# Linear attention and its neighbours: a split wait, a gate and half a unit in other places, the router's scores behind the first Silu

## What is computed

```python
# ffn0, on the layer-normed tokens xf
shared = jax.nn.silu(xf @ shared_w1.T) * (xf @ shared_w2.T) @ shared_w3.T
scores = jax.nn.sigmoid(xf @ router_w.T)
_, top_idx = jax.lax.top_k(scores + expert_bias, TOP_K)
...
return (shared + routed).reshape(b, s, d)

# gla, H = 4 heads, q/k of 64, v of 128 per head
q = split(x @ Wq.T, HQK); k = split(x @ Wk.T, HQK); v = split(x @ Wv.T, HV)
g = jax.nn.log_sigmoid((x @ Wgk1.T @ Wgk2.T + bgk2) * GATE_MULT) / GATE_NORM
o = gla_fused_chunk(q, k, v, g)      # S_t = diag(exp(g_t)) S_{t-1} + k_t v_t^T ; o_t = q_t^T S_t
o = o * jax.lax.rsqrt(jnp.mean(o * o, axis=-1, keepdims=True) + EPS) * rms_w
gate = jax.nn.silu(x @ Wg.T)
return o.reshape(B, N, DV) * gate @ Wout.T
```

## Time and profile before

| | us |
|---|---|
| timed runs, median (lowest to highest of 3) | 1657.66 (1654.03 to 1658.09) |
| profiled execution | 1649.87 |
| its span, first to last instruction | 1647.8 |
| PE busy | 1604.7 |
| DVE, ACT, POOL busy | 1181.8, 875.4, 706.5 |
| share of the chain that ended last: PE | 83% |

### The profile page before, as it was taken

How to read it: one execution, slowest core, us unless ns; L and a number is a source line. 1 busy time by engine, 2 the same in 40 slices (tenths; PEclk the granted TensorE clock), 3 DMA queues, 4 the chain that set the end, 5 groups by cost and what they waited for, 6 DMA issues and landing times.

```text
span 1647.8 us, 42417 instructions
## 1 busy us (share of the span) xinstructions
PE 1604.7 (97%) x15094; PEld 1082.7 (66%) x15095; DVE 1181.8 (72%) x2536; ACT 875.4 (53%) x1509; POOL 706.5 (43%) x660
## 2 busy tenths in 40 slices
PE   6999999999999999999999999999999999999998
PEld 3665566666666776765655666666657777777576
DVE  6677775666666666667866656666688879888886
ACT  5455543444376666664343334444376676675664
POOL 2342242433235455442332333334235567777343
PEclk9999999999999999999999999999999999999999
DMA  7132233333311211003210123333423033231001
GB/s 263 52 102 88 87 103 92 110 110 111 93 31 27 38 26 25 0 1 88 100 43 26 38 78 100 112 109 105 106 62 53 2 79 80 54 67 42 20 32 52
DMA packets 91304, 115.71 MB, mean 70 GB/s; under 512 B 9425, under 2 KB 76529, under 8 KB 91185
## 3 DMA queue, kind: packets, MB, share of 16 engines
q1 hardware_dynamic: 70832, 71.17, 15.2%
q0 software_dynamic: 20352, 42.88, 9.1%
HBM read 66.11 MB, written 47.90 MB: 69 GB/s over the span
## 4 chain that ended last, share of the span: by engine, by line
PE 83%; DVE 7%; ACT 5%; issue 3%; POOL 1%; DMA 1%; DVEq 0%; SPq 0%; ACTq 0%; POOLq 0%
PE ps L1965 19%; PE ps L1967 19%; PE ps L1966 18%; PE ps L2255 3%; PE ps L2254 3%; PE ps L2204 3%; PE ps L2205 3%; PE ps L1981 2%; PE ps L2176 2%; PE ps L2157 2%; PE ps L2349 1%; PE ps L2485 1%; PE ps L2519 1%; PE ps L2497 1%; PE ps L2311 1%
## 5 line engine op out<-in xcount | busy, mean ns | idle before, releaser
L778 POOL DMA_INDIRECT routed<-work x142 | 136.6, 962 | 235.7 <-DVE work L1638 230.6
L1965 PE MATMUL ps<-later_hi,work 128*128 (+1 forms) x632 | 203.3, 322 | 0.5 <-DVE work L1618 0.3
L1967 PE MATMUL ps<-later_hi,work 128*128 (+1 forms) x632 | 203.1, 321 | 0.0
L1966 PE MATMUL ps<-later_lo,work 128*128 (+1 forms) x632 | 203.1, 321 | 0.0
L1965 PE MATMUL ps<-xt_hi,wsh 128*128 128x512 f16 x508 | 192.6, 379 | 4.7 <-DVE work L1509 4.5
L1967 PE MATMUL ps<-xt_hi,wsh 128*128 128x512 f16 x508 | 192.5, 379 | 0.0
L1966 PE MATMUL ps<-xt_lo,wsh 128*128 128x512 f16 x508 | 192.5, 379 | 0.0
L951 ACT ACTIVATE work<-ps 128x512 f32<-128x512 f32 x128 | 76.4, 597 | 172.6 <-PE ps L1967 166.3
L1965 PE MATMUL ps<-wsh,work 128*128 128x256 f16 x512 | 139.5, 273 | 0.8 <-DVE work L1438 0.6
L1509 DVE SCALAR_TENSOR_TENSOR work<-ps,work 128x512 f32<-128x512 f32 x128 | 88.1, 689 | 72.1 <-ACT work L951 56.6
L1966 PE MATMUL ps<-wsh,work 128*128 128x256 f16 x512 | 139.5, 273 | 0.2 <-issue 0.2
(11 more groups left out here) (267 smaller groups left out, 4307.0 us busy)
## 6 DMA issues: line engine op xcount, KB each, us to landing
work<-expert_x SPq DMA_DIRECT2D x142, 129.0 KB
yg<-in_w_later SPq DMA_DIRECT2D x9, 496.0 KB
w1q<-in_w_later SPq DMA_DIRECT2D x9, 496.0 KB
yg<-in_w SPq DMA_DIRECT2D x16, 256.0 KB
values<-wsh SPq DMA_DIRECT2D x8, 512.0 KB, 4.1
later_hi<-values SPq DMA_DIRECT2D x16, 256.0 KB, 4.8
later_lo<-values SPq DMA_DIRECT2D x16, 256.0 KB, 5.2
out_x<-x SPq DMA_DIRECT2D x8, 512.0 KB, 3.0
```

The costliest lines, as they stand in the source:

```text
L778: nc.gpsimd.indirect_dma_start(routed[:, :], bass.IndirectOffsetOnAxis(m.homes[:, i:i + 1], 0), m.t_y[:, i % 4, :], None).then_inc(s[f"til ...
L1965: nc.tensor.matmul(out_, a[0], b[0], start=start, stop=False)
L1966: nc.tensor.matmul(out_, a[0], b[1], start=False, stop=False)
L1967: return nc.tensor.matmul(out_, a[1], b[0], start=False, stop=stop)
```

## The change

Five edits, and no change to what is computed:

- ACT, first sequence of both ffn0: `scores(0)` moves from ahead of Silu 0 to behind it.
- PE, gla: the one wait ahead of the states for both copies of the keys becomes one wait for the first copy ahead of c = 0 and one for the second ahead of c = 2.
- PE, last sequence of gla: the gate of c = 1 moves ahead of the wait for the turned keys' copy; the other three stay where the four were. ACT takes the gates' Silus in the order 1, 0, 2, 3.
- PE, last sequence: the first half of the next ffn0's unit 0 stays ahead of the turn of half 0; its second half moves behind it, ahead of the turn of half 1.
- `shared_unit` is cut into two calls of `shared_half`, `gate` becomes a function.

```diff
+        def gate_order(g):
+            return (1, 0, 2, 3) if is_last(g) else range(TPS)
...
-                    if is_first(g):
-                        scores(0)
-                    elif not is_last(g) and not is_second(g):
+                    if not is_first(g) and not is_last(g) and not is_second(g):
                         scores(g + 1)
...
+                        if is_first(g) and k == 0:
+                            scores(0)
...
-                    for c in range(TPS):
-                        act.wait_ge(s["gate_ready"], g * TPS + c + 1)
+                    for i, c in enumerate(gate_order(g)):
+                        act.wait_ge(s["gate_ready"], g * TPS + i + 1)
...
+                def gate(g, u, c):
+                    project(u, ps[:, GGATE[c], :], gg, 0, H * DV, c).then_inc(s["gate_ready"], 1)
...
+                    else:
+                        gate(g, u, gate_order(g)[0])
                     pe.wait_ge(s["kt_copied"], g + 1)
                     pe.wait_ge(s["v_copied"], (g + 1) * TPS)
-                    if not is_last(g):
-                        pe.wait_ge(s["qk_copied"], (g + 1) * 2 * GPAIR + GPAIR)
                     for c in range(TPS - 1):
                         at = c * GPAIR * DV
+                        if not is_last(g) and c != 1:
+                            pe.wait_ge(s["qk_copied"], (g + 1) * 2 * GPAIR + 1 + c // 2)
...
-                    for c in range(TPS):
+                    for c in gate_order(g)[1 if is_last(g) else 0:]:
                         if c == 2 and not is_last(g):
                             pe.wait_ge(s["exps_ready"], (g + 2) * 2)
-                        project(u, ps[:, GGATE[c], :], gg, 0, H * DV, c).then_inc(s["gate_ready"], 1)
+                        gate(g, u, c)
...
                         gate_left(1)
-                        shared_unit(n + 1, 0, 0, 0)
+                        shared_half(n + 1, 0, 0, 0, 0)
                     turn(0)
+                    if is_last(g) and unit_ahead(n + 1, 0):
+                        shared_half(n + 1, 0, 0, 0, 1).then_inc(S[n + 1]["up_ready"], 1)
```

More of the change, by code:

```diff
@@ L1988, in shared_unit, with shared_half @@
             def shared_unit(n, g, u, q):
[L1990 to L1995, removed]
+                shared_half(n, g, u, q, 0)
+                shared_half(n, g, u, q, 1).then_inc(S[n]["up_ready"], 1)
+            def shared_half(n, g, u, q, half):
+                for k in range(KT):
+                    w = both((wsh1, wsh2)[half], slice(k * HSH + q * P, k * HSH + (q + 1) * P))
+                    ins = mm3(ps[:, up_bank(g, q) + half, :], w, xt(u, k), k == 0, k == KT - 1)
+                return ins
             def opening_unit(n):
```

## The result

The changed kernel takes 1649.94 us (median of 6, 1645.48 to 1653.04) against 1657.09 of the kernel before (median of 6, 1654.03 to 1658.86): ratio 0.9958, 95% interval 0.9947 to 0.9970, so 7.15 us or 0.42% faster. The forecast was 1650.3 us with 7.35 us gained. The profiled execution took 1645.48 us, its span is 1643.4 us.

A forecast was written before the change was run, and what follows sets the result against it. TensorE was taken as the bound, busy 1604.7 of 1647.8 us, so only its gaps could be won. 2.0 + 2.3 + 1.4 + 1.65 = 7.35 us off 1657.66 gave 1650.3 us, range 1645.5 to 1655.5.

The forecast's parts named there:

- first opening: First ffn0: with scores behind Silu 0, unit 3 starts at 23.76 and not 25.74, gaining 2.0 us.
- split wait: States of the linear attention: waiting for the keys' copies separately gains 0.33 us at each of seven waits, 2.3 us.
- last sequence: Last linear-attention sequence: early gate and moved half unit start the output at 746.0 and not 747.41, gaining 1.4 us.
- second opening: Second ffn0: scores behind Silu 0 start unit 3 at 757.25 and not 760.30, 1.65 us beyond the last sequence's 1.4.
- (a): ACT table changes cost more than their load row; the first opening's 2.0 us falls to 0.1: 1652.2 us, chance 0.07.
- (b): DVE sets the pace where gaps close, in the last sequence and both openings: 5.1 us gained or some 3.8, chance 0.15.
- (c): At the states, the next wait ends as late and other gaps reopen: within 3 us of before, 1656, chance 0.09.
- (d): New wait amid the states stops PE 1.5 us in 7 sequences: term −10.2, time 1662.8 us, chance 0.04.
- the steady sequence: Sign in the linear attention: a steady sequence takes 35.9 us and not 36.22.
- the last sequence's gap gone: Sign at the last sequence's states: PE's idle is under 0.2 us.
- the wait at the first turn: Sign in the last sequence: a new PE idle of some 0.6 us stands before the first turn.
- the output nearer: Sign in the last sequence: the output starts 1.4 us nearer.

The follow-up runs named there:

- the repeat: The changed kernel timed again on another chip, against the kernel before: 1642.34 us beside 1648.95, ratio 0.9955.
- gate alone: Kernel before with only the last sequence's early gate, unit 0 whole ahead of the first turn: 1648.57 us beside 1648.95, ratio 0.9993.
- half unit alone: Kernel before with only the second half of the last sequence's shared unit moved behind the first turn: 1650.89 us beside 1652.60, ratio 0.9988.
- both openings: Kernel before with only the router's scores behind Silu 0 in both ffn phases: 1648.99 us beside 1652.60, ratio 0.9978.
- the earlier Silu: Changed kernel with the last sequence's early-gate Silu between ACT's two squares: 1640.88 us, kernel before beside it 1648.95, ratio 0.9952.
- first opening alone: Kernel before with only the scores behind Silu 0 in the first ffn0: 1647.97 us beside 1649.06, ratio 0.9990.
- split alone: Kernel before with only the wait for the keys' copies split in two: 1647.35 us beside 1649.06, ratio 0.9988.

## Why the prediction was right, point by point

**The sum.** 7.35 us was forecast and 7.15 measured; the terms' own sum is 6.85. That the totals agree to 0.2 us is in part luck: the interval of the 7.15 is 5.0 to 8.8 us, and the repeat gave 6.6. Two terms were 0.3 us too high, and what happened outside the edited places is larger than these differences. The terms, by the leads:

| term | forecast | measured |
|---|---|---|
| first opening | 2.0 | 1.7 (1.5 to 2.35) |
| split wait | 2.3 | 2.0 |
| last sequence | 1.4 | 1.55 |
| second opening | 1.65 | 1.60 |

**First opening.** Right in mechanism, and slightly too good in size. Unit 2 starts with no wait at all, but unit 3 still waits, 0.40 us in the changed kernel where the prediction had at most 0.2, and it starts at 24.00 where 23.8 was forecast. In the other four profiles of the new order the idle figure is 0, 0, 0.19 and 0.46: the earlier unit 1 begins (18.69, 18.61, 18.12 and 17.94 us; 18.26 in the changed kernel's profile), the longer PE waits. ACT's first load began at 17.24 in the changed kernel and at 16.85 in the earlier trace rows; with 6.76 behind it, 16.85 gives 23.61, so PE's own 23.76 would have been right for that execution, with no wait. The size came from one execution: there the old order cost 2.12 us ahead of the Silu's load, and in seven other profiles it cost 1.51 to 2.35, mostly about 1.7. The step that failed is that it took as given how late the router was for ACT.

**A part of it is given back later, sometimes.** In the changed kernel's profile the lead falls from 1.71 us at 85 us to 1.19 at 155 (at 153.58 the router waits 0.28 us for the low half of a tile) to 0.73 at 250 and to −0.16 at 252. The waits of PE at that place are for data coming by DMA; its timeline there:

```profile
250.82 0.41 PE L2163 MATMUL ps<-consts,work 128*128 128x128 f32 x2 [0.70 <-DMA work<-expert_x]
251.79 0.44 PE L2163 MATMUL ps<-consts,work 128*128 128x128 f32 x2 [0.56 <-DMA work<-expert_x]
```

These are the experts' first gathered tiles. The stretch from PE's matmul at 240 us in the profile of before to the one at 256 takes 15.9 us in six of the eight profiles of the old order, and 16.5 and 16.3 in the other two (gate alone, half unit alone). With the new order it is 16.8 in the changed kernel, 16.5 in its repeat, 16.7 with both openings, 16.3 with the earlier Silu and 15.9 with the first opening alone. So up to 0.9 us of a lead can end as a wait for that transfer. It did in four of five profiles with the new order, but also in two of eight without it, so it is not shown that the edit is the cause. What decides stays open, and so does the rest of the 1.35 us lost between 155 and 252 us.

**Split wait.** The 0.33 us of a steady sequence is right: 35.90 and 36.23. The mis-sized term is the count: "with seven such waits" was read off a row of totals, and seven gains need seven sequences with the same next step. In the first one the next wait, for POOL's lower half of the scores, ends as late as the old one did, and six sequences gained. The prediction said that what comes next starts at the same distance behind the states, and looked only at the sequence it had rows for. The timelines of the changed kernel show the new wait:

```profile
481.04 0.23 PE L2360 MATMUL ps<-w1q,work 128*128 128x128 f16 x1 [0.32 <-POOL work L799]
```

```profile
478.85 2.13 POOL L799 TENSOR_TENSOR work<-work 128x1024 f16<-128x1024 f32 x1
```

**Last sequence.** The gate filled the gap as foreseen, PE waits at the first turn (0.48 us against some 0.6), and the second turn needs no wait beyond its cover: 743.95 − 742.73 = 1.22 us to the output with no idle figure. 1.55 us was gained against 1.4. The prediction followed ACT and DVE step by step past the two turns, and that is why it did not simply add the filled 1.30 us and the moved half unit's share, which alone give 1.02 and 1.29 and would sum to 2.31.

**Second opening.** Silu 0 runs at 744.78 right behind ACT's copies, product 0 at 750.57, product 1 3.93 us later, and unit 3 at 755.24: 11.29 us behind the output product and not 12.89. The term is right to 0.05 us.

**The rivals.** (a), a dearer table change, is refuted: the earlier trace rows showed 0.01 us between load and Silu, and the three loads of the changed kernel show 0.01 and 0.02. The Trainium skill (page ScalarE: Activation LUTs, section What ACT_TABLE_LOAD costs) adds a drain of about 1380 ns to each switch; the trace does not agree: from the end of Silu 0 to the start of Silu 1 the rows of the changed kernel leave 0.05 us beside the two loads and the sigmoid. (b), DVE as the pace, is the one with some truth. DVE released the 0.40 us at unit 3 and the 0.48 at the first turn, but it took nothing like half of the terms; the experiment with the earlier Silu gave the later one back. (c), a split that does nothing, holds for one sequence of seven. (d), a price for the wait in the middle of the states, is refuted at 0: the states are 1.53 us in one row with it and without it, and the period shrank by all that the copy's wait had been. Its sum in the prediction was also off: a stop of 1.46 us in each of seven sequences takes 10.2 us from the 2.3 us gained, so the term would be −7.9 and not −10.2, and the time some 1660.5 and not 1662.8.

**The level.** The forecast took the median of the timed runs, 1657.66, and not the profiled 1649.87 as its base. The kernel before gave 1657.09 beside the changed one, but three of those six executions are the ones the forecast started from, so the level was known and is no test of it. The later sessions, 1648.95 to 1652.60, show that the level belongs to the session, and only the gain carries over.

**The signs.** Most came as named: the steady sequence, the last sequence's gap gone, the wait at the first turn, the output nearer. Two did not. Unit 3 stood 0.40 us idle and not 0.2 at most. And PE's total idle time in a single profile was 39.0 us where about 37 was foreseen; the repeat of the changed kernel has 1641.1 − 1603.5 = 37.6. A total over 1643 us carries 2 us and more of chance from places that the change does not touch.

## What to carry to other kernels

A wait that the trace shows n times is worth n times its gap only if the next thing on the path is as early in all n; look at the first and the last turn of a loop apart, since a step of another engine can come later there. Where two edits fill gaps behind one chain of another engine, follow that chain through both: here 1.02 and 1.29 us made 1.55, and moving the chain's start gave another 1.0. And a gain of a few tenths of a per cent is best read as the lead of one trace over another at fixed instructions, just ahead of and just behind the edit, because the time of the whole can't resolve it.

## What the runs showed of the hardware

- A wait that is already met costs nothing that can be seen on PE, even between matmuls of one form: 24 records in 1.53 us with and without it, and no gap inside. A table load on ACT costs 1.28 us and up to 0.02 more, also three times within 5 us.
- The windowed attention (some 1342 to 1500 us) differs from execution to execution by up to 3.9 us with the same PE instructions (157.8 us in the changed kernel, 161.7 in the first opening alone). In the first opening alone PE stopped inside one run of small matmuls, as its timeline shows:

```profile
1393.44 0.74 PE L2488 MATMUL ps<-work,wsh 32*64 32x64 f32 x34 [1.38 <-issue]
```

  No instruction of another engine releases it. Four such stops took 3.2 us in that kernel, and four took 1.9 us in the repeat of the changed kernel. The split alone has none of over 0.3 us at these places. In the trace the stops fall beside transfers of 16 KB on the instruction queue that started later than in the profile without them: in the first opening alone the four stops begin 0.1 to 1.0 us behind the end of such a transfer, and against PE's own progress the first three transfers started 2.7 to 3.5 us later than in the split alone, the fourth 0.3. A late fetch of instructions is thus a possible cause, but it is not shown; no run was made for it. Most of the repeat's fall from a lead of 9.45 us at 1275 us to 6.76 at the end lies in this stretch (2.6 us).
